# State sums by accumulated transposes in a decoder's state-space stage, with one more channel block's convolution on TensorE

## What is computed

```
for i in range(4):
    h = rms(x, norm_w[i])
    xi, z = split(h @ W_in[i].T, 2)                  # 512 channels each
    xc = silu(conv_b[i] + sum(xp[:, k:k+L] * conv_w[i][:, k] for k in range(4)))
    delta, Bm, Cm = split(xc @ W_x[i].T, [64, 80])
    delta = softplus(delta @ W_dt[i].T + b_dt[i])
    deltaA = exp(delta[..., None] * -exp(A_log[i]))  # 16 states per channel
    BX = (delta * xc)[..., None] * Bm[:, :, None, :]
    _, hs = associative_scan(combine, (deltaA, BX))  # h = deltaA * h + BX
    y = einsum('bldn,bln->bld', hs, Cm) + D[i] * xc
    x = x + (y * silu(z)) @ W_out[i].T
```

## Time and profile before

| | |
|---|---|
| three runs | 1286.21, 1291.24, 1297.13 us, median 1291.24 us |
| profiled execution, own time | 1294.53 us |
| its span, first to last instruction | 1292.8 us |
| busy: PE, DVE, ACT, POOL | 1132.0, 1051.4, 829.8, 785.5 us |
| rounds 1 to 6 | 447 to 969 us of the span, two rounds in 174.1 us |

### The profile page before, as it was taken

How to read it: one execution, slowest core, us unless ns; L and a number is a source line. 1 busy time by engine, 2 the same in 40 slices (tenths; PEclk the granted TensorE clock), 3 DMA queues, 4 the chain that set the end, 5 groups by cost and what they waited for, 6 DMA issues and landing times.

```text
span 1292.8 us, 17441 instructions
## 1 busy us (share of the span) xinstructions
PE 1132.0 (88%) x5930; PEld 665.7 (51%) x5930; DVE 1051.4 (81%) x1637; ACT 829.8 (64%) x1827; POOL 785.5 (61%) x660
## 2 busy tenths in 40 slices
PE   7799888878859998998998989989989689999874
PEld 3455555544435454554554545545545346676644
DVE  4577777676589999999999999999999975776566
ACT  1555555555466786777677767877676437788754
POOL 6001111200389898998998999989989951553105
PEclk9899999989779999999998999989999799999875
DMA  6000002000510600503304106023041012100000
GB/s 210 13 12 13 12 13 73 1 1 3 201 43 0 228 22 7 198 17 110 140 1 183 39 1 249 1 83 138 1 180 58 1 42 59 34 19 17 1 2 25
DMA packets 22141, 79.13 MB, mean 61 GB/s; under 512 B 4935, under 2 KB 8847, under 8 KB 21138
## 3 DMA queue, kind: packets, MB, share of 16 engines
q1 hardware_dynamic: 22054, 78.02, 17.4%
HBM read 76.77 MB, written 1.24 MB: 60 GB/s over the span
## 4 chain that ended last, share of the span: by engine, by line
PE 41%; DVE 30%; POOL 14%; ACT 8%; issue 6%; DMA 1%; SPq 0%; ACTq 0%; DVEq 0%; POOLq 0%
PE ps L672 36%; DVE ps L2065 10%; POOL arena L1979 9%; DVE arena L2068 4%; PE ps L741 4%; DVE arena L2070 4%; POOL arena L1991 3%; DVE hstat L1198 2%; ACT ps L1862 2%; DVE arena L2028 2%; DVE arena L1174 1%; ACT L667 1%; ACT arena L930 1%; DVE arena L1164 1%; DMA arena<-in_exb 1%
## 5 line engine op out<-in xcount | busy, mean ns | idle before, releaser
L672 PE MATMUL ps<-arena 128*32 128x100 f32 (+8 forms) x3300 | 518.4, 381 | 73.4 <-ACT arena L930 14.6
L1979 POOL TENSOR_TENSOR arena<-arena 128x1600 f32<-128x1600 f32 x128 | 456.4, 3581 | 34.1 <-DVE ps L2065 25.9
L672 PEld LDWEIGHTS ps<-arena 128*32 128x32 f32 (+6 forms) x3300 | 262.2, 146 | 297.0 <-issue 114.4
L672 PE MATMUL ps<-arena,ident 128*128 128x400 f32 x1024 | 385.4, 527 | 29.5 <-POOL arena L1991 20.0
L1862 ACT ACTIVATE ps<-arena 128x400 f32<-128x400 f32 x512 | 282.9, 590 | 184.4 <-DVE arena L2068 151.2
L2065 DVE TENSOR_TENSOR_SCAN ps<-ps,arena 128x800 f32<-128x800 f32 x176 | 320.6, 1822 | 22.6 <-ACT ps L1862 17.1
L672 PEld LDWEIGHTS ps<-arena,ident 128*128 128x128 f32 x1024 | 201.6, 200 | 196.4 <-issue 28.5
L639 POOL TENSOR_SCALAR stat<-stat 100x1 f32<-100x1 f32 (+1 forms) x44 | 8.4, 191 | 388.0 <-DVE stat L620 387.1
L2068 DVE TENSOR_TENSOR arena<-ps,arena 128x800 f32<-128x800 f32 x176 | 174.5, 991 | 6.0
L1991 POOL TENSOR_TENSOR arena<-arena 128x1600 f32<-128x1600 f32 x40 | 143.0, 3575 | 17.0 <-DVE arena L2070 16.8
L2070 DVE TENSOR_TENSOR_SCAN arena<-ps,arena 128x800 f32<-128x800 f32 x80 | 140.4, 1804 | 1.0 <-ACT ps L1862 0.8
(11 more groups left out here) (197 smaller groups left out, 1044.5 us busy)
## 6 DMA issues: line engine op xcount, KB each, us to landing
arena<-bc_scratch SPq DMA_DIRECT2D x64, 800.0 KB, 6.5
arena<-in_ctxT SPq DMA_DIRECT2D x16, 361.0 KB, 4.0
arena<-in_w_in SPq DMA_DIRECT2D x4, 1024.0 KB, 5.1
arena<-in_expT SPq DMA_DIRECT2D x1, 2048.0 KB, 12.9
arena<-in_w_out SPq DMA_DIRECT2D x4, 512.0 KB, 3.3
arena<-in_mask SPq DMA_DIRECT2D x8, 141.0 KB
arena<-in_xT SPq DMA_DIRECT2D x2, 400.0 KB, 4.4
x_tok<-in_x_tok SPq DMA_DIRECT2D x1, 800.0 KB
```

Of the source, the lines that this page charges most:

```text
L672: return nc.tensor.matmul(outp, lhsT, rhs, start=first, stop=last)
L1979: nc.gpsimd.tensor_tensor(bx[:, unit % BX].rearrange("p (j t) -> p j t", j=SEGMENT), bbc[:, nq].rearrange("p (j t) -> p j t", j=SEGMENT), ...
```

## The change

1. For blocks 0, 1 and 2 the sum over states is made on its side. `pm_reduce` first clears a bank of 100 x 512 with a matmul of zeros (one per block), and then adds 16 transposes per unit (four states, four batch rows): 128x100 is the stationary side, the 128x128 identity moves, and the result accumulates as tokens x channels. Block 3 keeps the identity matmuls.
2. When a block's four units are in, ScalarE copies the 100x512 result to SBUF (`am_turned_sums`, steps 5, 9 and 13, waiting for `m_red`), TensorE adds D * xc and turns it back with four transposes (`pm_back`, steps 6, 10, 14, waiting for `m_yt`), and `vm_y` waits for `m_yb`. The copy lies in parts of `y2` not yet in use. `vm_y` moves from steps 5, 10, 13 to 7, 11, 15; block 3's stays.
3. Block 1's convolution goes the way of blocks 2 and 3: four more taps at ScalarE's step 6, the raw copy at 9, four matmuls at TensorE's step 10 (product Y1), bias at ScalarE's step 10. `vm_conv` keeps three instructions, block 0's.
4. X1 is made before X0 in `PREP`.

```diff
-    "aG": (5, 6),
+    "aG": {2: 5, 3: 6, 1: 6},
-    "vY": (5, 10, 13, 16),
+    "vY": (7, 11, 15, 16),
+    "aYT": (5, 9, 13),
+    "pY": (6, 10, 14),
+    "pY1": 10,
+    "aR1": 9,
+    "aY1": 10,
...
-        taps = mam.take(2, DC, P)
+        taps = mam.take(3, DC, P)
...
+        def turned_rows(c):
+            at = y2_at + min((c + 1) * GT, CD * GT - GB * P)
+            return arena[:, at:at + GB * P]
...
             wait_c(pe, unit)
+            if c < CD - 1:
+                if nq == 0:
+                    mm(ps[0:S, 4 + c % 2, :], identb[0:1, 1:S + 1],
+                       identb[0:1, :].rearrange("p (o t) -> p o t", o=1).to_broadcast([1, GB, P]), True, False)
+                for j in range(SEGMENT):
+                    for b in range(GB):
+                        last = nc.tensor.matmul(ps[0:S, 4 + c % 2, b * P:(b + 1) * P],
+                                                hs[:, unit % HS, j * GT + b * S:j * GT + (b + 1) * S], ident[:, :],
+                                                is_transpose=True, start=False,
+                                                stop=nq == NQ - 1 and j == SEGMENT - 1 and b == GB - 1)
+                last.then_inc(m_red, 1)
+                return
...
+        def pm_back(pe, m, c):
+
+            pe.wait_ge(m_yt, (CD - 1) * m + c + 1)
+            pe.wait_ge(m_skip, m // G + 1)
+            o = ps[:, 4 + c % 2, 0:GT]
+            mm(o, dgd[:, c], xc[m % G][:, c], True, False)
+            for b in range(GB):
+                last = nc.tensor.matmul(o[:, b * S:(b + 1) * S], turned_rows(c)[0:S, b * P:(b + 1) * P], ident[0:S, 0:S],
+                                        is_transpose=True, start=False, stop=b == GB - 1)
+            last.then_inc(m_yb, 1)
...
+        def am_turned_sums(act, m, c):
+
+            act.wait_ge(m_red, UNITS * m + NQ * (c + 1))
+            nc.scalar.activation(turned_rows(c)[0:S, :], ps[0:S, 4 + c % 2, :], ACT.Copy).then_inc(m_yt, 1)
...
-        def vm_conv(dve, m, g, c0):
-
-            dve.wait_ge(m_acc, 2 * m + CD)
+        def vm_conv(dve, m, g):
+
+            dve.wait_ge(m_acc, m + CD)
+            n = "X0"
             for s in range(1, DC):
-                for c in (c0, c0 + 1):
...
-            dve.wait_ge(m_red, UNITS * m + NQ * (c + 1))
+            if c < CD - 1:
+                dve.wait_ge(m_yb, (CD - 1) * m + c + 1)
+            else:
+                dve.wait_ge(m_red, UNITS * m + NQ * CD)
             nc.vector.tensor_tensor(y2[:, c], ps[:, 4 + c % 2, 0:GT], sz[g][:, c], ALU.mult).then_inc(m_y2, 1)
```

More of the change, by code:

```diff
@@ L297, in decoder @@
         delta[1] = mam.take(CD, GT)
[L298 to L299 removed]
+        taps = mam.take(3, DC, P)
+        mam.at += CD * GT - 3 * DC * P
         dx = mam.take(CD, GT)
@@ L302, in decoder @@
         hs = mam.take(HS, SEGMENT * GT)
+        y2_at = mam.at
         y2 = mam.take(CD, GT)
@@ L1372, in decoder @@
         m_taps = sem("m_taps")
+        m_yt, m_yb = sem("m_yt"), sem("m_yb")
         ROUNDS = G * NL
-        PREP = (["T0", "T1", "X2", "X3", "Y2", "Y3", "X0", "X1", "DB"] + [f"D{c}" for c in range(CD)]
+        PREP = (["T0", "T1", "X2", "X3", "Y2", "Y3", "X1", "X0", "Y1", "DB"] + [f"D{c}" for c in range(CD)]
                 + [f"X{e}" for e in range(CD, 2 * CD)])
@@ L1546, in pm_conv @@
             for s in range(DC):
-                last = mm(y3[:, :, s:S], taps[:, c - 2, DC - 1 - s], x3[:, :, 0:S - s], s == 0, s == DC - 1)
+                last = mm(y3[:, :, s:S], taps[:, c - 1, DC - 1 - s], x3[:, :, 0:S - s], s == 0, s == DC - 1)
             last.then_inc(m_full, 1)
@@ L1669, in mam_pe @@
                                 pm_conv(pe, m + 1, c)
-                        for e in (0, 1, *range(CD, 2 * CD)):
+                        for e in (1, 0, *range(CD, 2 * CD)):
                             if u == AT["pX"][e]:
                                 pm_in(pe, m + 1, e)
+                        if u == AT["pY1"]:
+                            pm_conv(pe, m + 1, 1)
                     if UNITS * m + u >= LAG_R:
                         pm_reduce(pe, UNITS * m + u - LAG_R)
+                    for c in range(CD - 1):
+                        if u == AT["pY"][c]:
+                            pm_back(pe, m, c)
                     if m + 1 < ROUNDS:
@@ L1789, in am_taps @@
             if m and c == 2:
-                p_full(act, m, "Y3")
+                p_full(act, m, "Y1")
             for k in range(DC):
-                last = nc.scalar.activation(taps[:, c - 2, k], ident[:, :], ACT.Identity,
+                last = nc.scalar.activation(taps[:, c - 1, k], ident[:, :], ACT.Identity,
                                             scale=cvw[:, DC * c + k:DC * c + k + 1])
-            if c == 3:
+            if c == 1:
                 last.then_inc(m_taps, 1)
+        def am_turned_sums(act, m, c):
+            act.wait_ge(m_red, UNITS * m + NQ * (c + 1))
+            nc.scalar.activation(turned_rows(c)[0:S, :], ps[0:S, 4 + c % 2, :], ACT.Copy).then_inc(m_yt, 1)
         def am_z(act, m, g, c):
@@ L1807, in am_silu @@
                 return
-            for names, c in ((("Y2", "Y3"), 2), (("X0", "X1"), 0)):
+            for names, c in ((("Y2", "Y3"), 2), (("X0", "Y1"), 0)):
                 for n in names:
@@ L1873, in mam_act @@
                         am_unit(act, UNITS * m + u)
+                    for c in range(CD - 1):
+                        if u == AT["aYT"][c]:
+                            am_turned_sums(act, m, c)
                     for c in range(CD):
@@ L1894, in mam_act @@
                         am_turned(act, m + 1)
+                    for c in (2, 3, 1):
+                        if u == AT["aG"][c] and (m == 0 or g == 1):
+                            am_taps(act, m, l + g, c)
                     for c in (2, 3):
-                        if u == AT["aG"][c - 2] and (m == 0 or g == 1):
-                            am_taps(act, m, l + g, c)
                         if u == AT["aX"]:
@@ L1902, in mam_act @@
                             am_conv_out(act, m + 1, ng, c)
-                    for c in range(2):
-                        if u == AT["aC"]:
-                            am_conv(act, m + 1, ng, c)
+                    if u == AT["aR1"]:
+                        am_raw_x(act, m + 1, ng, 1)
+                    if u == AT["aC"]:
+                        am_conv(act, m + 1, ng, 0)
+                    if u == AT["aY1"]:
+                        am_conv_out(act, m + 1, ng, 1)
                     for c in range(CD):
@@ L2104, in mam_dve @@
                         if u == AT["vC"]:
-                            vm_conv(dve, m + 1, ng, 0)
+                            vm_conv(dve, m + 1, ng)
             vm_y(dve, ROUNDS - 1, CD - 1)
```

17 lines of the change are left out of this document (7 added, 10 removed).

## The result

| | before | after |
|---|---|---|
| median of 20 runs each | 1289.09 us (1280.26 to 1297.54) | 1300.18 us (1293.41 to 1307.52) |
| profiled execution's own time | 1294.53 | 1294.88 |
| its span | 1292.8 | 1293.1 |

The changed kernel is slower by 0.7%: ratio 1.0072, 95% interval 1.0052 to 1.0092. That is less than the 1% that I had said a measurement of this kernel can tell; with 20 runs of each the interval is narrower than that.

What follows compares the result with a forecast made beforehand. VectorE was taken as the bound, with ScalarE's order without slack at some steps. Three even rounds at +1.0 us and four with taps at +2.9 gave +14.6, forecast 1305 us, slower by 1.1%, range 1280 to 1322 (own 1294 to 1316).

Steps and rivals of the forecast that it cites:

- my signs: Expected in the profile: two middle rounds 177 to 179 us, TensorE's clock 0.95, unit 14 waiting 2 to 3 us.
- TensorE's part: 16 transposes take 1.76 us instead of 2.68; TensorE falls from 81 to about 75 us a round, alone buying nothing.
- VectorE's part: Three of six convolution instructions remain on VectorE, taking 1.6 us off a round (bounds 1.2 and 1.8).
- Step 9 and unit 10: ScalarE's copy of block 1's sums waits for unit 7's reduction; VectorE waits 1.0 us before unit 10 every round.
- Steps 5 to 7, odd rounds: One copy and four more taps on ScalarE delay unit 7, with block 0's `vm_y` behind: 2.2 us more.
- Step 13 and unit 14: Copy of block 2's sums delays unit 14: 0.9 us at full clock, 2.1 (even) and 3.4 (odd) as clock falls.
- Unit 15: The second softplus pair leaves a 0.35 us wait instead of 0.73 (even) and 1.3 (odd): gains 0.4 and 0.9.
- Rival 1: VectorE keeps its saving, no ScalarE waits before units 10 and 14: 1275 us, faster; chance 0.2.
- Rival 2: TensorE's clock stays full at step 13, or recovers before D0; unit 14 waits 0.9 us: 1291 us, no change; chance 0.14.
- Rival 3: Clock falls once more in the reductions of units 2 to 5, some 2.5 us later each round: 1322 us; chance 0.16.

Runs made afterwards that it cites:

- conv_only: Changed kernel with block 1's convolution kept on TensorE but all sums over states by identity matmuls, no copies or turns back: 1274.91 us, 0.9869 of before.
- late_taps: Changed kernel with second and third copies at ScalarE's steps 10 and 15, block 1's `vm_y` at 12, taps at 4, 5, 6: 1282.89 us, 0.9914 of before.
- after_fill_both: Changed kernel with idle matmuls in both TensorE pauses, before the W_x product and unit 12's wait: 1291.96 us, 1.0016 of before.
- late_taps_fill_both: late_taps with idle matmuls in both TensorE pauses: 1282.30 us, 0.9938 of before.
- nocopy_fill12: Changed kernel without copies and turns back (sums of blocks 0 to 2 left out), plus twelve idle matmuls before unit 12's wait: 1281.40 us, 0.9933 of before.
- copies: conv_only plus three unused 32x400 copies at ScalarE's steps 5, 9 and 13, `vm_y` at the changed kernel's steps: 1341.55 us, 1.0402 of before.

## Why the prediction was right, and where it was not

**The forecast.** 1305 us, slower by 1.1%, was forecast; 1300.18, slower by 0.7%, was measured. The direction, the engine and the places were right: VectorE's saving of 1.6 us a round is spent on waits for ScalarE at units 10 and 14 and, in odd rounds, at units 6 and 7. Over six rounds +11.7 was forecast and +8.4 measured; against the median of before +13.8 (from the first three runs) and +11.1 (from twenty). Some of my signs were missed: two middle rounds take 176.6 us, not 177 to 179, their clock is 0.98, not 0.95, and unit 14 waits 1.3 and 2.0 us, not 2 to 3.

**TensorE's part.** 1.76 us for 16 transposes: 1.74 to 1.84 at full clock. 75 us a round: 75.01 and 74.75. That it buys nothing by itself was right, and was too mild: it opened pauses. They slowed TensorE no more than the pauses before had (clock 0.98 and 0.97), but conv_only shows what was there to be had, 1.00.

**VectorE's part.** 1.6 us off: 3.45 to 1.85.

**Step 9 and unit 10.** 1.0 us: 1.20 and 0.85. ScalarE's copy waits 0.80 and 0.44 for the transposes of unit 7, as worked out.

**Steps 5 to 7, odd rounds.** Units 6 and 7 together wait 0.99 + 1.81 = 2.80, against 0.65 before, so 2.15 more; 2.2 was forecast. late_taps shows the taps' share alone: unit 7's wait is 0.66 with them at steps 4 and 5.

**Step 13 and unit 14, the step that failed in size.** I took over from before where the clock falls: ahead of unit 11's reduction. The waits of 2.1 and 3.4 us in my sum were an estimate, from the 4.65 and 5.49 us that unit 11's eight records took before instead of 2.85; no run shows them. Measured are 1.26 and 2.01. In round 4 the W_x product, D0, D1 and unit 11 all ran at full clock and the copy at step 13 found its sums ready. In round 5 it was the W_x product that took 4.59 us, after a pause of 2.78; unit 11 itself ran at full clock. Which of the two happens changed from round to round and not with even and odd; unit 14's wait was at most 2.01 in any round, and 3.4 in none. With the clock full it is 1.5 (after_fill_both), where I had 0.9.

**Unit 15, the other half of the same miss.** I counted gains of 0.4 and 0.9 there, down to a wait of 0.35. In round 5 it was 0.23, from 1.27 before. In round 4 it rose from 0.73 to 1.77: the pause before unit 12 and the half clock behind it delay D2 and D3, the second softplus pair waits 1.36 us for them, and unit 15 for that pair. The even round came out 1.6 us longer instead of 1.0, the odd one 0.9 instead of 2.9. For rounds 4 and 5, with the measured waits in place of mine, my own sum gives: even -1.6 + 1.2 + 1.1 + 1.0 = +1.7, odd -1.6 + 2.15 + 0.85 + 0.8 - 1.0 = +1.2. The ledger was right; the price and the place of the clock were not. That the total came so near is in part luck: unit 14 was charged 0.85 and 1.4 us too much, and in the even round unit 15 1.4 too little.

**Rival 1** (VectorE keeps its saving) did not occur in the changed kernel. conv_only comes nearest to what it describes, and its 16.7 us (1274.91 against 1291.57) are close to the 16 that I had worked out for it. That is partly chance: the taps' wait of 1.2 us at unit 7 came, which the rival leaves out, and the full clock made up for it. The change as made has the copies besides.

**Rival 2** (the clock stays full at step 13) was half true: at unit 11 it did stay full, which was my sign for this rival, but it fell elsewhere in the same round. after_fill_both is this rival as it was meant, and gives 1.0016, no change, as I had said of it.

**Rival 3** (the clock falls once more, around step 7) did not occur in the changed kernel. From 754 to 780 us, a stretch with five whole groups of 16 transposes, the granted clock is 1.00 with TensorE busy 20.23 of 26 us; in late_taps_fill_both it was 1.00 over 86 us, a whole round with twelve of them. But in nocopy_fill12 it is what happened: in rounds 2, 4 and 5 the reduction of unit 5 took 3.21, 3.62 and 2.92 us instead of 1.95. What transposes by themselves do to the clock these runs do not show: it stayed full over whole rounds with twelve groups, it fell among groups in nocopy_fill12, and none shows transposes alone.

**What stays open.** How much the kernel before would gain with its own pauses filled was not run, so the clock's share in the difference between before and after is not known. How the 15.3 us that the turned sums cost at full clock divide between copies, turns back and `vm_y` was not taken apart. Nor was it tried to hand the copies to an engine other than ScalarE.

## What to carry to other kernels

Before an engine's work is made cheaper, ask what waits for it. Here TensorE had 6 us a round taken off and hardly anything had been waiting for it at those steps, while the copies that this needed stood in the fixed order of the one engine that VectorE does wait for. The copies put between two halves of this double-buffered producer cost their own wait for their source (0.80 us at step 9 of round 4, 2 us on average in copies) besides their 0.6 us, so such an instruction belongs behind a step at which that source has long been ready; moving two of three there was worth 1.2% (from 1.0072 to 0.9948). And a change with two parts is to be run as two: one part of this one is worth 1.3% alone, 1.6% with its taps spread, and the other hid it.
